# The last two chunks of a graph kernel's first edge pass, in an order written out by hand on TensorE, VectorE and ScalarE

## The chip, the cores and the metric

The kernel runs on one core of one Trainium2 chip. The metric is the device time of one execution in microseconds (us), as the median of several runs. TensorE is PE in the profile, VectorE is DVE, ScalarE is ACT, GpSimd is POOL and SyncE is SP. Each engine has its own instruction stream, and the streams meet at semaphores.

## The reference

Two graph layers follow each other on 3125 nodes with 64 channels and 100000 edges sorted by destination, each with a residual and a layer norm. The first layer is what the change touches:

```python
h1, h2, h3, h4 = (_node_proj(x, W, b, node_type) for W, b in ...)
w5e = einsum('mf,mfh->mh', edge_feat, W5[edge_type]) + b5[edge_type]
num = sum(h3[edge_dst] * (h4[edge_src] + w5e), axis=-1)
score = softmax((num / sqrt(16))[:, None], axis=-1)[:, 0]
msg = score[:, None] * (h2[edge_src] + w5e)
out = h1 + segment_sum(msg, edge_dst, num_segments=n)
...
x = layernorm(x + out)
```

The second layer gathers the rows of this new `x` by `edge_src`, so nothing of it can be gathered before the first layer's sums are complete.

## The kernel before, in words

The program has a preparation, an edge pass over 98 chunks (stage 0, the first layer), a short part on the nodes (sums of each node fetched, layer norm), a second edge pass over 98 chunks (stage 1, the second layer) and an end part. A chunk is 512 edges of the first half of the edge list beside 512 of the second half, so that 128 partitions hold two times 64 channels. Chunk c has the parity s = c % 2 and the round r = c // 2; most tiles exist twice, one for each parity, and semaphores of the pair count rounds. The last two chunks are 96 (s = 0) and 97 (s = 1).

In stage 0 a chunk goes through these steps, each a function called with `chunk_of(c)`:

- POOL, `gather0` (L509): six or eight indirect DMAs of rows into a ring of eight buffers (`rows0_0`, `rows0_1`, and six in `block1`, which the profile prints as `rows` and `block`).
- PE, `project0`: one matmul of the masked features by `w5` (L779, printed as x2), then the gathered rows are transposed and added to it (L753, L758), which is what `q4_ready` announces; and the start values `inj` are transposed (L788, `injT`).
- DVE, `products`: a scan that carries the row of h3 from edge to edge (L1078, `h3_ready`, needs `injT`), then the product with `q_sum` (L1083, `prod_ready`, needs `q4_ready`).
- PE, `numerator` (L805) transposes the product, and `difference` (L753, L758) adds the other half of the rows to `q_sum`.
- DVE, `score_parts` (L1057, L1060, L1063): sums of channels, maximum, difference. ACT, `exponents` (L598). DVE, `probabilities` (L1088, L1090, L1093). ACT, `widen` (L604), spreads the probability over the channels. PE, `turn_prob` (L814), transposes it.
- DVE, `message_sums` (L1099, L1105): the product with `q2_sb` (copied by ACT, `copy_q2`, L617) and the scan of sums, `run`. It needs `keep_late`, which ACT copies in `copy_keep` (L611).
- PE, `turn_run` (L825), transposes `run`. ACT, `store0` (L628, L630), copies it and issues the store to `d_run0`.

The order on each engine is that in which the code calls the functions: a loop over c with offsets, so that in one turn an engine works on up to four neighbouring chunks. DVE's turn c is `score_parts(c-1)`, `mask(c+1)`, `products(c)`, `probabilities(c-1)`, `message_sums(c-2)`; PE's is `project0(c+1)`, `numerator(c)`, `difference(c)`, `turn_prob(c-1)`, `turn_run(c-2)`; ACT's is `exponents(c-1)`, `copy_keep(c)`, `widen(c-1)`, `copy_q2(c)`, `store0(c-2)`. In every turn but the last ones PE also does 75 matmuls of `pick0` (L770) and DVE some 12 comparisons (L1051) for the rows that are picked by matmul instead of gathered.

When all stores of stage 0 have landed, POOL fetches the sums of each node (L541, 25 indirect DMAs), DVE and ACT norm them in five groups, SP writes `d_x1`, and POOL's gathers of stage 1 (`gather1`, L519) start.

Of the kernel before, what the change touches and what calls it, by code (L numbers as in the profile page):

```python
# [33 lines left out]
CHUNKS = 2 * -(-N_EDGES // (4 * CH))  # L34
# [36 lines left out]
def gnn_program(nc, t, out):  # L71
# [3 lines left out]
    with ctx:  # L75
# [221 lines left out]
        def chunk_of(c):  # L297
            return (c % 2, c // 2, c) if 0 <= c < CHUNKS else None

        def tiles_of(c):  # L300

            return PE_J if c % 2 == 0 else TILES
# [8 lines left out]
        def wait(eng, semaphore, count):  # L311

            if count > 0:
                eng.wait_ge(semaphore, count)
# [247 lines left out]
        def _(act):  # L562
# [56 lines left out]
            def copy_picked(u):  # L619

                act.wait_ge(picked[u % 2], u // 2 + 1)
                wait(act, q2_ready[0], u - 1)
                act.activation(picked_sb[u % 2], p_pick[u % 2], ACT.Copy).then_inc(own_ready[u % 2], 1)

            def store0(s, r, c):
                act.wait_ge(runT[s], r + 1)
                wait(act, stored[s], 16 * r)
                act.activation(stage0[s][:, :, :].rearrange("p j c -> p (j c)"), p_out0[:, :], ACT.Copy).then_inc(staged[s], 1)  # L628
                act.wait_ge(staged[s], r + 1)
                act.dma_start(d_run0[bass.ds(2 * CH * c, 2 * CH), :].rearrange("(p j h) c -> p j (h c)", j=TILES, h=2),  # L630
                              stage0[s][:, :, :]).then_inc(stored[s], 16)

            copy_picked(0)
            for c in range(CHUNKS + 2):
                for work, d in ((exponents, -1), (copy_keep, 0), (widen, -1), (copy_q2, 0)):
                    if chunk_of(c + d):
                        work(*chunk_of(c + d))
                if c % 2 == 0 and c // 2 + 1 < PICKS:
                    copy_picked(c // 2 + 1)
                if chunk_of(c - 2):  # L640
                    store0(*chunk_of(c - 2))

            def square_and_root(g, first):

                act.wait_ge(s_square, first + g + 1)
                act.activation(sq[:, g * GT:(g + 1) * GT, :], centred[:, g * GT:(g + 1) * GT, :], ACT.Square).then_inc(s_squared, 1)
                act.wait_ge(s_var, first + g + 1)
                act.activation(std[:, g * GT:(g + 1) * GT], var[:, g * GT:(g + 1) * GT], ACT.Sqrt).then_inc(s_sqrt, 1)
# [72 lines left out]
        def _(pe):  # L721
# [27 lines left out]
            def add_rows(s, c, which):  # L749

                rows = [ring[c % RING][:, j, :, :].rearrange("p h c -> p (h c)") for j in range(TILES)]
                for j in range(tiles_of(c)):
                    ins = pe.matmul(q_sum[s][:, j:CH:TILES], rows[j][:, which:4 * C:2], ident[:, :], is_transpose=True,  # L753
                                    start=False, stop=True, skip_group_check=True)
                if c % 2 == 0:
                    u = c // 2
                    for h in range(2):
                        ins = pe.matmul(q_sum[s][:, PE_J:CH:TILES], sel[:, which, (1 - h) * C:(3 - h) * C], picked_sb[u % 2][:, h * P:(h + 1) * P],  # L758
                                        start=False, stop=True, skip_group_check=True)
                return ins  # L760
# [14 lines left out]
            def project0(s, r, c):  # L775

                pe.wait_ge(masked[s], r + 1)
                wait(pe, q2_copied[s], r)
                pe.matmul(q_sum[s], w5[:, :], featm[s][:, :], start=True, stop=True)  # L779
                pe.wait_ge(got_rows[c % RING], 16 * 2 * tiles_of(c) * (c // RING + 1))  # L780
                if c % 2 == 0:
                    pe.wait_ge(own_ready[c // 2 % 2], c // 4 + 1)
                add_rows(s, c, 1).then_inc(q4_ready[s], 1)
                pe.wait_ge(inj_in[s], 16 * (r + 1))
                if c > 0:
                    pe.wait_ge(h3_ready[1 - s], r + s)
                for j in range(TILES):
                    ins = pe.matmul(p_inj[:, j:CH:TILES], inj[s][:, j, :], ident[:, :], is_transpose=True,  # L788
                                    start=True, stop=True)
                ins.then_inc(injT[s], 1)  # L790
# [38 lines left out]
            pe.wait_ge(s_left, 2)  # L829
            for half in range(2):  # L830
                pick0(0, half)
            for c in range(-1, CHUNKS + 2):
                u, half = (c + 3) // 2, (c + 3) % 2
                if u < PICKS:
                    pick0(u, half)
                for work, d in ((project0, 1), (numerator, 0), (difference, 0), (turn_prob, -1), (turn_run, -2)):
                    if chunk_of(c + d):
                        work(*chunk_of(c + d))

            def project1(s, r, c):  # L840

# [75 lines left out]
        def _(dve):  # L917
# [126 lines left out]
            def one_hot0(u, half):  # L1044

                s = u % 2
                if half == 0:
                    dve.wait_ge(slots_in[u % PICK_SLOTS], 16 * (u // PICK_SLOTS + 1))
                    wait(dve, picked[s], u // 2)
                for k in range(half * NT_FIRST, NT if half else NT_FIRST):  # L1050
                    ins = dve.tensor_scalar(hot0[s][:, k, :], pick_slots[u % PICK_SLOTS][0:NP, :], pick_of[:, k:k + 1], None, ALU.is_equal)  # L1051
                ins.then_inc(hot_ready[s], 1)
# [16 lines left out]
                dve.scalar_tensor_tensor(featm[s][:, :], types[s][:, :], type_of_row[:, :], feat[s][:, :],  # L1069
                                         ALU.is_equal, ALU.mult).then_inc(masked[s], 1)  # L1070

            def products(s, r, c):

                dve.wait_ge(keep_in[s], 32 * (r + 1))
                dve.wait_ge(injT[s], r + 1)
                if c > 0:
                    dve.wait_ge(h3_ready[1 - s], r + s)
                dve.tensor_tensor_scan(h3d[s][:, :], keep[s][:, :], p_inj[:, :], h3d[1 - s][:, CH - 1:CH],  # L1078
                                       ALU.mult, ALU.add).then_inc(h3_ready[s], 1)
                dve.wait_ge(h3_ready[s], r + 1)  # L1080
                dve.wait_ge(q4_ready[s], r + 1)
                wait(dve, num_ready[s], r)
                dve.scalar_tensor_tensor(prod[s][:, :], h3d[s][:, :], 0.25, q_sum[s], ALU.mult, ALU.mult).then_inc(prod_ready[s], 1)  # L1083
# [23 lines left out]

            for u, half in ((0, 0), (0, 1), (1, 0)):
                one_hot0(u, half)
            for c in range(-1, CHUNKS + 2):  # L1110
                for work, d in ((score_parts, -1), (mask, 1), (products, 0), (probabilities, -1), (message_sums, -2)):
                    if chunk_of(c + d):
                        work(*chunk_of(c + d))
                u, half = (c + 4) // 2, c % 2
                if u < PICKS:
                    one_hot0(u, half)

            def layer_norm(src, g, first):

# [205 lines left out]
```

## Time and profile before

| | |
|---|---|
| median of 3 runs | 1893.9 us (1891.12 to 1894.66) |
| profiled execution, its own time | 1900.41 us |
| its span in the trace | 1898.6 us |
| busy: PE, DVE, POOL, ACT | 1611.0, 1673.0, 1334.5, 758.3 us |
| mean granted TensorE clock | 0.952 of full speed |

The span is the time from the first to the last instruction in the trace; times in the trace's rows count from its start. The profiled execution is 1.8 us longer than its span and 6.5 us longer than the median of the runs. Busy shares are means over stages with different limits. For a change at one place only that place's rows tell what is waited for.

### The profile page before, as it was taken

To read this page: it belongs to the slowest core of one execution; us is meant where nothing else is said; L and a number is where in the kernel's file an instruction comes from. 1 tells how busy PE (TensorE), PEld (TensorE's weight loads), DVE (VectorE), ACT (ScalarE), POOL (GpSimd) and SP (SyncE) were. 2 spreads that over 40 slices of the span, in tenths; PEclk is the share of its full clock that TensorE was granted. 3 is DMA by queue.
4 is the path that set the end of the run, shared out by engine and by line. 5 is a ranking of instruction groups with operands and counts; after the bars stand their busy time and mean duration, and the time that the engine had idled before them with its cause. 6 is when DMAs were issued, how large, how long until landed. Compare 5 with 4: busy or idle time off the path is not lost.

```text
span 1898.6 us, 32478 instructions
## 1 busy us (share of the span) xinstructions
PE 1611.0 (85%) x10331; PEld 1182.0 (62%) x10331; DVE 1673.0 (88%) x3845; ACT 758.3 (40%) x1438; POOL 1334.5 (70%) x1391
## 2 busy tenths in 40 slices
PE   4406999999999999999982399999999999999936
PEld 3305888888888888888772155555555555555525
DVE  4333999999999999999987589999999999999976
ACT  3100233332323333233321156665665665665632
POOL 3557777777777777777773677777777777777742
PEclk9998999999999999999996699999999999999955
DMA  9782555556565665655552256666666666666631
GB/s 288 233 327 86 167 168 173 171 172 178 166 177 169 171 177 167 178 163 173 165 161 55 58 145 187 189 184 181 177 189 187 187 185 183 176 190 184 182 101 38
DMA packets 220337, 323.22 MB, mean 170 GB/s; under 512 B 65697, under 2 KB 127706, under 8 KB 220039
## 3 DMA queue, kind: packets, MB, share of 16 engines
q1 hardware_dynamic: 116096, 146.04, 25.2%
q0 software_dynamic: 44464, 70.87, 17.9%
q10 hardware_dynamic: 59608, 104.24, 15.2%
q8 instruction: 84, 1.38, 0.3%
q14 instruction: 85, 0.70, 0.1%
HBM read 186.93 MB, written 134.02 MB: 169 GB/s over the span
## 4 chain that ended last, share of the span: by engine, by line
POOL 61%; issue 21%; PE 6%; DVE 5%; DMA 4%; SPq 2%; ACT 1%; ACTq 0%; DVEq 0%; POOLq 0%
POOL rows L519 29%; POOL block L509 22%; POOL rows L509 8%; PE bank L729 2%; POOL typed L541 1%; DMA d_inj<-zeros 1%; POOL d_inj L532 1%; SPq L387 1%; PE wide L912 1%; PE wide L770 1%; DMA w_nodes<-in_b 1%; DVE edge_lists L1051 1%; DVE h3d L1078 0%; DVE run L1105 0%; DVE late L1051 0%
## 5 line engine op out<-in xcount | busy, mean ns | idle before, releaser
L519 POOL DMA_INDIRECT rows<-d_x,idx x588 | 557.2, 948 | 189.2 <-issue 179.0
L509 POOL DMA_INDIRECT block<-d_h,idx x504 | 490.6, 973 | 153.7 <-issue 153.4
L866 PE MATMUL wide<-late,ntype_i 125*128 125x512 bf16 x975 | 220.8, 382 | 51.5 <-DVE ntype_i L1180 51.5
L770 PE MATMUL wide<-late,typed 125*128 125x256 bf16 x1250 | 209.6, 274 | 62.7 <-DVE late L1051 62.6
L611 ACT ACTIVATE keep_late<-keep 128x512 bf16<-128x512 bf16 x98 | 61.8, 630 | 428.8 <-DVE run L1105 428.8
L509 POOL DMA_INDIRECT rows<-d_h,idx x182 | 176.7, 971 | 70.5 <-issue 55.2
L866 PE MATMUL wide<-edge_lists,ntype_i 125*128 125x512 bf16 x936 | 210.0, 379 | 0.0
L770 PE MATMUL wide<-edge_lists,typed 125*128 125x256 bf16 x1200 | 201.6, 275 | 3.8 <-DVE edge_lists L1051 3.3
L866 PEld LDWEIGHTS wide<-late,ntype_i 125*128 125x128 bf16 x975 | 96.3, 99 | 157.9 <-DVE ntype_i L1180 51.9
L877 PE MATMUL wide<-ident,block 128*128 128x128 f32 x784 | 141.8, 306 | 38.3 <-DVE block L1220 29.5
L770 PEld LDWEIGHTS wide<-late,typed 125*128 125x128 bf16 x1250 | 120.3, 98 | 82.3 <-issue 59.0
L770 PE MATMUL wide<-late,ntype_i 125*128 125x256 bf16 x625 | 171.2, 274 | 0.0
L770 PE MATMUL wide<-edge_lists,ntype_i 125*128 125x256 bf16 x600 | 164.5, 274 | 0.0
L866 PEld LDWEIGHTS wide<-edge_lists,ntype_i 125*128 125x128 bf16 x936 | 92.1, 98 | 100.0
L877 PEld LDWEIGHTS wide<-ident,block 128*128 128x128 f32 x784 | 110.3, 209 | 62.5 <-DVE block L1220 47.4
L1078 DVE TENSOR_TENSOR_SCAN h3d<-keep,h3d,bank 128x512 f32<-128x512 bf16 x98 | 124.8, 1274 | 25.5 <-PE bank L788 25.5
L680 ACT ACTIVATE bank<-prob_wide 128x512 f32<-128x512 f32 x98 | 59.0, 602 | 214.1 <-DVE block L1220 210.7
L1051 DVE TENSOR_SCALAR late<-zeros,pick_of 125x256 bf16<-125x256 f16 x625 | 128.3, 299 | 4.0 <-DMA zeros<-d_pick 4.0
L770 PEld LDWEIGHTS wide<-edge_lists,typed 125*128 125x128 bf16 x1200 | 115.5, 99 | 23.2 <-DVE edge_lists L1051 9.4
L1195 DVE TENSOR_TENSOR_SCAN h3d<-bank,h3d,keep 128x511 f32<-128x511 f32 x98 | 125.5, 1281 | 3.5
L1105 DVE TENSOR_TENSOR_SCAN run<-keep_late,run,bank 128x512 f32<-128x512 bf16 x98 | 125.4, 1280 | 3.5
L1215 DVE TENSOR_TENSOR_SCAN block<-bank,block 128x512 f32<-128x512 f32 x98 | 124.3, 1268 | 1.1 <-ACT bank L680 1.1
(207 smaller groups left out, 3453.7 us busy)
## 6 DMA issues: line engine op xcount, KB each, us to landing
d_run<-block ACTq DMA_DIRECT2D x98, 512.0 KB
d_inj<-zeros SPq DMA_DIRECT2D x28, 896.0 KB, 16.9
inj<-d_inj SPq DMA_DIRECT2D x98, 256.0 KB
d_run<-stage ACTq DMA_DIRECT2D x98, 256.0 KB
feat<-in_ea16x3T SPq DMA_DIRECT2D x196, 96.0 KB
types<-d_type SPq DMA_DIRECT2D x196, 64.0 KB
keep<-d_keep SPq DMA_DIRECT2D x196, 64.0 KB
keep<-d_pen SPq DMA_DIRECT2D x196, 64.0 KB
```

What stands on the lines that cost most here:

```text
L509: pool.indirect_dma_start(out=ring[c % RING][:, j, h, :], out_offset=None, in_=d_h24, in_offset=bass.IndirectOffsetOnAxis(ap=idx[:, c, at: ...
L519: pool.indirect_dma_start(out=rows1[c % RING1][:, j, h, :], out_offset=None, in_=d_x1, in_offset=bass.IndirectOffsetOnAxis(ap=idx[:, c, at ...
L611: act.activation(keep_late[s][:, :], keep[s][:, :], ACT.Copy).then_inc(keep_copied[s], 1)
L680: act.activation(p_decay[:, :], up[s], ACT.Exp, scale=-1.0).then_inc(decay_ready[s], 1)
L770: ins = pe.matmul(p_pick[s], table0[n][:, k, :], hot0[s][:, k, :], start=(k == 0 and n == 0), stop=(k == NT - 1 and n == 2), skip_group_ch ...
L866: ins = pe.matmul(p_hot[s], table[q][:, SPLIT * k:SPLIT * (k + 1), :].rearrange("p b c -> p (b c)"), hot[s][:, k, :], start=(k == 0 and q ...
L877: ins = pe.matmul(p_out1[:, q * CH + j * P:q * CH + (j + 1) * P], src[:, j:CH:TILES], ident[:, :], is_transpose=True, start=True, stop=True)
L1051: ins = dve.tensor_scalar(hot0[s][:, k, :], pick_slots[u % PICK_SLOTS][0:NP, :], pick_of[:, k:k + 1], None, ALU.is_equal)
L1078: dve.tensor_tensor_scan(h3d[s][:, :], keep[s][:, :], p_inj[:, :], h3d[1 - s][:, CH - 1:CH], ALU.mult, ALU.add).then_inc(h3_ready[s], 1)
L1105: dve.tensor_tensor_scan(run[s][:, :], keep_late[s][:, :], p_prob[:, :], run[1 - s][:, CH - 1:CH], ALU.mult, ALU.add).then_inc(run_ready[s ...
L1195: dve.tensor_tensor_scan(before[s][:, 1:CH], p_m[c % 3][:, 0:CH - 1], keep[s][:, 1:CH], before[s][:, 0:1], ALU.max, ALU.add).then_inc(befo ...
L1215: dve.tensor_tensor_scan(run_s[s][:, :], p_decay[:, :], expm[s][:, :], run_s[1 - s][:, CH - 1:CH], ALU.mult, ALU.add).then_inc(s_run[s], 1)
```

## The change

The three loops end two turns earlier on their upper side and the last turns are written out as one list for each engine; `CHUNKS - back` is the chunk, so back 1 is chunk 97 and back 2 is chunk 96. Two functions are split so that their halves can stand apart: `turn_inj` is the second half of `project0`, and `expand` is the first half (the scan of h3) of `products`. Up to and with turn 95 each engine's order is as it was. No instruction is added or removed.

```diff
@@ ScalarE
-            for c in range(CHUNKS + 2):
+            for c in range(CHUNKS - 2):
...
+            for work, back in ((exponents, 3), (copy_keep, 2), (widen, 3), (copy_q2, 2), (store0, 4), (exponents, 2), (widen, 2),
+                               (copy_keep, 1), (copy_q2, 1), (exponents, 1), (store0, 3), (widen, 1), (store0, 2), (store0, 1)):
+                work(*chunk_of(CHUNKS - back))
@@ TensorE
                 add_rows(s, c, 1).then_inc(q4_ready[s], 1)
+
+            def turn_inj(s, r, c):
+
                 pe.wait_ge(inj_in[s], 16 * (r + 1))
...
-            for c in range(-1, CHUNKS + 2):
+            for c in range(-1, CHUNKS - 2):
...
-                for work, d in ((project0, 1), (numerator, 0), (difference, 0), (turn_prob, -1), (turn_run, -2)):
+                for work, d in ((project0, 1), (turn_inj, 1), (numerator, 0), (difference, 0), (turn_prob, -1), (turn_run, -2)):
...
+            for work, back in ((numerator, 2), (difference, 2), (turn_prob, 3), (turn_run, 4), (turn_inj, 1), (project0, 1),
+                               (turn_prob, 2), (numerator, 1), (difference, 1), (turn_run, 3), (turn_run, 2), (turn_prob, 1), (turn_run, 1)):
+                work(*chunk_of(CHUNKS - back))
@@ VectorE
-            def products(s, r, c):
+            def expand(s, r, c):
...
+            def products(s, r, c):
+
                 dve.wait_ge(h3_ready[s], r + 1)
...
-            for c in range(-1, CHUNKS + 2):
-                for work, d in ((score_parts, -1), (mask, 1), (products, 0), (probabilities, -1), (message_sums, -2)):
+            for c in range(-1, CHUNKS - 2):
+                for work, d in ((score_parts, -1), (mask, 1), (expand, 0), (products, 0), (probabilities, -1), (message_sums, -2)):
...
+            for work, back in ((score_parts, 3), (mask, 1), (expand, 2), (products, 2), (probabilities, 3), (message_sums, 4),
+                               (score_parts, 2), (expand, 1), (probabilities, 2), (message_sums, 3), (products, 1),
+                               (message_sums, 2), (score_parts, 1), (probabilities, 1), (message_sums, 1)):
+                work(*chunk_of(CHUNKS - back))
```

On PE, behind `turn_run` of chunk 93 (which is the transpose of `run1`), the program before goes on with the matmul of chunk 97's features by `w5` and its last gathered rows (`rows0_1`), and only then with chunk 96's numerator (`prod0`):

```order
L825 MATMUL bank3<-ident,run1 128x128 x4
L779 MATMUL wide0<-featm1,w5 128x512
L753 MATMUL wide0<-ident,rows0_1 128x128 x4
L788 MATMUL bank0<-ident,inj1 128x128 x4
L805 MATMUL bank1<-ident,prod0 128x128 x4
L753 MATMUL wide0<-ident,rows0_0 128x128 x3
L758 MATMUL wide0<-msg1,sel 128x128 x2
L814 MATMUL bank2<-ident,prob_wide1 128x128 x4
L825 MATMUL bank3<-ident,run0 128x128 x4
```

The same place in the changed program (its line numbers are higher by 3 to 6: L820 is `turn_prob`, L831 `turn_run`, L811 `numerator`, L794 `turn_inj`, L782 the matmul by `w5`):

```order
L831 MATMUL bank3<-ident,run1 128x128 x4
L811 MATMUL bank1<-ident,prod0 128x128 x4
L756 MATMUL wide0<-ident,rows0_0 128x128 x3
L761 MATMUL wide0<-msg1,sel 128x128 x2
L820 MATMUL bank2<-ident,prob_wide1 128x128 x4
L831 MATMUL bank3<-ident,run0 128x128 x4
L794 MATMUL bank0<-ident,inj1 128x128 x4
L782 MATMUL wide0<-featm1,w5 128x512
L756 MATMUL wide0<-ident,rows0_1 128x128 x4
```

All of chunk 97's PE work has moved behind the four pieces that belong to chunks 94, 95 and 96, and the transpose of `inj1` stands ahead of chunk 97's rows.

On DVE, behind `message_sums` of chunk 94 (`run0`), the program before has chunk 96's scores, chunk 97's scan and product, chunk 96's probabilities and chunk 95's message sums (`run1`):

```order
L1057 TENSOR_REDUCE score0<-bank1 128x8
L1060 TENSOR_REDUCE top0<-score0 128x8
L1063 TENSOR_TENSOR diff0<-score0,top0 128x8
L1078 SCALAR_TENSOR_TENSOR h3d1<-keep1,h3d0,bank0 128x512
L1083 SCALAR_TENSOR_TENSOR prod1<-h3d1,wide0 128x512
L1088 TENSOR_REDUCE total0<-expo0 128x8
L1090 RECIPROCAL inv0<-total0 128x8
L1093 TENSOR_TENSOR prob0<-expo0,inv0 128x8
L1099 TENSOR_TENSOR bank2<-bank2,q2_sb1 128x512
L1105 SCALAR_TENSOR_TENSOR run1<-keep_late1,run0,bank2 128x512
L1057 TENSOR_REDUCE score1<-bank1 128x8
```

The same place in the changed program (L1087 is the scan of h3, L1095 the product, L1111 and L1117 are `message_sums`):

```order
L1066 TENSOR_REDUCE score0<-bank1 128x8
L1069 TENSOR_REDUCE top0<-score0 128x8
L1072 TENSOR_TENSOR diff0<-score0,top0 128x8
L1087 SCALAR_TENSOR_TENSOR h3d1<-keep1,h3d0,bank0 128x512
L1100 TENSOR_REDUCE total0<-expo0 128x8
L1102 RECIPROCAL inv0<-total0 128x8
L1105 TENSOR_TENSOR prob0<-expo0,inv0 128x8
L1111 TENSOR_TENSOR bank2<-bank2,q2_sb1 128x512
L1117 SCALAR_TENSOR_TENSOR run1<-keep_late1,run0,bank2 128x512
L1095 SCALAR_TENSOR_TENSOR prod1<-h3d1,wide0 128x512
L1111 TENSOR_TENSOR bank2<-bank2,q2_sb0 128x512
L1117 SCALAR_TENSOR_TENSOR run0<-keep_late0,run1,bank2 128x512
```

The product of chunk 97 has moved behind `run1` of chunk 95, and chunk 96's message sums stand ahead of chunk 97's scores.

On ACT, the program before from the exponentials of chunk 96 (`expo0`) to the end of the stage:

```order
L598 ACTIVATE expo0<-diff0 128x8
L611 ACTIVATE keep_late1<-keep1 128x512
L604 ACTIVATE prob_wide0<-prob0 128x512
L617 ACTIVATE q2_sb1<-wide0 128x512
L628 ACTIVATE stage0_1<-bank3 128x512
L630 DMA d_run0<-stage0_1 128x512
L598 ACTIVATE expo1<-diff1 128x8
L604 ACTIVATE prob_wide1<-prob1 128x512
```

And in the changed program, with the same line numbers:

```order
L598 ACTIVATE expo0<-diff0 128x8
L604 ACTIVATE prob_wide0<-prob0 128x512
L611 ACTIVATE keep_late1<-keep1 128x512
L617 ACTIVATE q2_sb1<-wide0 128x512
L598 ACTIVATE expo1<-diff1 128x8
L628 ACTIVATE stage0_1<-bank3 128x512
L630 DMA d_run0<-stage0_1 128x512
L604 ACTIVATE prob_wide1<-prob1 128x512
```

Chunk 96's probabilities no longer stand behind the copy of `keep_late1`, and chunk 97's exponentials stand ahead of the store of chunk 95.

## Rows read from the trace of the kernel before

**Rows 1.** The page, part 4: the chain that ended last, by engine.

```profile
POOL 61%; issue 21%; PE 6%; DVE 5%; DMA 4%; SPq 2%; ACT 1%; ACTq 0%; DVEq 0%; POOLq 0%
```

**Rows 2.** The page, part 5, stage 1's gathers: busy, mean ns | idle before.

```profile
L519 POOL DMA_INDIRECT rows<-d_x,idx x588 | 557.2, 948 | 189.2 <-issue 179.0
```

**Rows 3.** The timeline of POOL around the end of stage 0: start, duration (us).

```profile
999.29 0.95 POOL L509 DMA_INDIRECT rows<-d_h,idx  x1 [0.30 <-issue]
...
1028.85 0.95 POOL L541 DMA_INDIRECT typed<-d_run,last_i  x1 [28.61 <-DMA d_run<-stage]
...
1073.14 1.08 POOL L519 DMA_INDIRECT rows<-d_x,idx  x1 [10.21 <-DMA d_x<-typed]
```

**Rows 4.** The timeline of PE in the loop of stage 0.

```profile
973.50 1.02 PE L779 MATMUL wide<-featm,w 128*128 128x512 f32 x2
...
975.46 0.60 PE L788 MATMUL bank<-ident,inj 128*128 128x128 f32 x4
975.90 0.65 PE L805 MATMUL bank<-ident,prod 128*128 128x128 f32 x4
976.38 0.64 PE L753 MATMUL wide<-ident,block 128*128 128x128 f32 x4
```

**Rows 5.** The timeline of PE at the end of stage 0.

```profile
1003.82 1.13 PE L753 MATMUL wide<-ident,rows 128*128 128x128 f32 x4 [5.72 <-DMA rows<-d_h,idx]
1004.75 1.06 PE L788 MATMUL bank<-ident,inj 128*128 128x128 f32 x4
1005.60 1.06 PE L805 MATMUL bank<-ident,prod 128*128 128x128 f32 x4
...
1021.10 1.09 PE L814 MATMUL bank<-ident,prob_wide 128*128 128x128 f32 x4 [4.17 <-DVE run L1105]
...
1024.30 1.13 PE L825 MATMUL bank<-ident,run 128*128 128x128 f32 x4 [1.25 <-DVE run L1105]
```

**Rows 6.** The timeline of DVE at the end of stage 0.

```profile
998.15 0.69 DVE L1083 SCALAR_TENSOR_TENSOR prod<-h3d,wide 128x512 f32<-128x512 f32 x1
...
999.99 1.28 DVE L1105 TENSOR_TENSOR_SCAN run<-keep_late,run,bank 128x512 f32<-128x512 bf16 x1
1006.70 0.69 DVE L1057 TENSOR_REDUCE score<-bank 128x8 f32<-128x512 f32 x1 [5.43 <-PE bank L805]
...
1011.14 0.16 DVE L1088 TENSOR_REDUCE total<-expo 128x8 f32<-128x8 f32 x1 [1.41 <-ACT expo L598]
...
1011.58 0.17 DVE L1093 TENSOR_TENSOR prob<-expo,inv 128x8 f32<-128x8 f32 x1
...
1012.39 1.28 DVE L1105 TENSOR_TENSOR_SCAN run<-keep_late,run,bank 128x512 f32<-128x512 bf16 x1
1013.59 0.67 DVE L1057 TENSOR_REDUCE score<-bank 128x8 f32<-128x512 f32 x1
...
1014.48 0.17 DVE L1063 TENSOR_TENSOR diff<-score,top 128x8 f32<-128x8 f32 x1
...
1022.23 0.70 DVE L1099 TENSOR_TENSOR bank<-bank,q_sb 128x512 f32<-128x512 f32 x1 [1.27 <-PE bank L814]
1022.96 1.28 DVE L1105 TENSOR_TENSOR_SCAN run<-keep_late,run,bank 128x512 f32<-128x512 bf16 x1
```

**Rows 7.** The timeline of ACT at the end of stage 0 (ACTq: its DMA issue).

```profile
1001.90 0.61 ACT L604 ACTIVATE prob_wide<-prob 128x512 f32<-128x512 f32 x1
...
1009.90 0.60 ACT L628 ACTIVATE stage<-bank 128x512 f32<-128x512 f32 x1 [1.11 <-PE bank L825]
...
1010.90 0.21 ACT L598 ACTIVATE expo<-diff 128x8 f32<-128x8 f32 x1 [0.40 <-ACT stage L628]
...
1026.09 0.33 ACTq L630 DMA_DIRECT2D d_run<-stage  x1
```

**Rows 8.** Stretches of 1 us: length, busy of PE, PEld, DVE, ACT, POOL, granted clock, DMA share, GB/s.

```profile
1004.00:1005.00 1.00, 1.00 (x6) 1.00 (x7) 0.00 (x0) 0.00 (x0) 0.00 (x0) 0.50 0.00 0
...
1010.00:1011.00 1.00, 1.00 (x8) 0.82 (x7) 0.00 (x0) 0.60 (x2) 0.00 (x0) 1.00 0.00 0
```

## The prediction

> **What bounds the kernel now.** I read the chain that ended last first: POOL and the time in which it merely issues are most of it [rows 1]. Stage 1's gathers explain why: POOL sat idle for 189.2 us around them, 179.0 us of it plain issue time [rows 2], and the remaining 10.2 us is one wait, that of its first gather for `d_x1` at 1073.14 [rows 3]. So in stage 1 POOL never waits for another engine, and whatever lets it start earlier is kept to the end. In front of it POOL stands still for 28.61 us, from its last gather of stage 0 (999.29) to its first fetch of node sums (1028.85), which waits for the last store [rows 3]. This hole is what the change can shorten. What fills it is read from the timelines of PE, DVE and ACT.
>
> The last gathered rows let PE go on at 1003.82 after 5.72 us of idleness [rows 5]. In those 5.72 us chunk 96's product was long there (998.15 plus 0.69, so 998.84 [rows 6]), but its numerator stood behind chunk 97's rows and started at 1005.60 [rows 5]. Hence DVE got chunk 96's scores to work on at 1006.70, after 5.43 us idle [rows 6]. Its exponentials then stood behind a store on ACT (copy at 1009.90, exponentials 1.00 us later, at 1010.90 [rows 7]), and DVE took them up at 1011.14 [rows 6]. Chunk 97's way from there was message sums at 1022.23, last transpose 1024.30, last store issued at 1026.09 [rows 5 to 7].
>
> **The change, step by step.** Nothing is added; instructions trade places. I follow the changed order with durations of the rows, twice: at full TensorE clock and at half. A group of four transposes starts 0.46 us after the one before at full clock (975.46, 975.90, 976.38) and itself lasts 0.60 to 0.65 [rows 4]; at half clock the pace is 0.86 (0.93 and 0.85 in the rows) and the length 1.06 to 1.13 [rows 5]. Below, the first number is full clock, the second half.
>
> 1. Up to DVE's `run` of chunk 94 all is as before: it ends at 999.99 + 1.28 = 1001.27 [rows 6].
> 2. PE does chunk 96's numerator at 998.90, as soon as the product is there, inside the wait for rows. Done by 999.6 or 1000.0. Its cover is that wait; without it, it would cost one group.
> 3. DVE takes chunk 96's scores right behind 1001.27; maximum and difference end 1.06 us later (1013.59 to 1014.65 [rows 6]), at 1002.33. Before, this began at 1006.70.
> 4. ACT's `widen` of chunk 95 ends at 1002.51, unmoved [rows 7]. PE: `turn_prob(95)` 1002.57, `turn_run(94)` 1003.03 / 1003.43, `turn_inj(97)` 1003.49 / 1004.29, ending 1004.09 / 1005.35. Behind it the matmul by `w5`: 1.05 us at full clock (1.02 plus issue [rows 4]); at half clock the trace has none, and I bound it between 1.05 and twice that. Then chunk 97's rows, which have landed at 1003.82 anyway, ready at 1005.65 / 1008.40. Before, they were added from 1003.82.
> 5. This is the wait that is added: DVE's scan `expand(97)` needs `turn_inj(97)`, and `probabilities(96)` and `message_sums(95)` are queued behind it. It starts at 1004.12 / 1005.38 and ends 1.28 us later, 1005.40 / 1006.66. DVE idles some 2 to 3 us there.
> 6. ACT stores chunk 94 from 1003.72 / 1004.53, and its exponentials of chunk 96 end 1.21 us later, 1004.93 / 1005.74. That is under the scan of step 5, so the store ahead of them costs nothing here; had the scan ended earlier, 0.9 us would show.
> 7. DVE needs 2.53 us from chunk 96's total to the end of chunk 95's `run` (1011.14 to 1012.39 + 1.28 [rows 6]): 1007.93 / 1009.19. Chunk 97's product follows with 0.69: 1008.62 / 1009.88. Its rows were ready 2.3 / 0.8 us before, so the late `w5` stays hidden, at either bound.
> 8. `widen(96)` ends at 1006.67 / 1007.9 and PE waits for `run` of chunk 95: `turn_prob(96)` 1008.05 / 1009.30, ending 1008.65 / 1010.39. DVE's `message_sums(96)` takes 2.01 (1022.23 to 1024.24 [rows 6]): 1010.69 / 1012.43. PE meanwhile does numerator and difference of 97 and `turn_run(95)`, until 1010.25 / 1012.94.
> 9. Scores of 97, 1.06: 1011.75 / 1013.49. Exponentials: 1011.99 / 1013.73. Now ACT stores chunk 95 in front of `widen(97)`, again 1.00 us [rows 7], of which DVE's probabilities (0.61, 1011.14 to 1011.75 [rows 6]) hide 0.6. `widen(97)` ends 1013.63 / 1015.37.
> 10. `turn_prob(97)` from 1013.69 / 1015.43, 0.60 / 1.09 long; `message_sums(97)` 2.01 plus 0.03: 1016.33 / 1018.56; last `turn_run` 0.06 later, 0.65 / 1.13 long: 1017.04 / 1019.75; store issued 0.66 later (1025.43 to 1026.09 [rows 5, 7]): 1017.70 / 1020.41.
>
> Against 1026.09 that is 8.4 us earlier at full clock throughout and 5.7 us at half clock throughout.
>
> **Which clock.** In the trace the granted clock was 0.50 (1.2 GHz) at 1004 to 1005, after PE had stood idle for 5.72 us, and back at 1.00 (2.4 GHz) at 1010 to 1011, after it had worked from 1003.82 on [rows 5, 8]. In the changed order the long hole has chunk 96's numerator and difference in it, and the next work starts at 1002.57. So I take full clock up to `turn_run(95)`, and half clock for the last three groups, which stand between gaps of 2 us and more as those at 1021.10 and 1024.30 did (1.09 and 1.13 us long [rows 5]). That is the full-clock line until `turn_prob(97)`, plus 0.49 on it and 0.48 on the last `turn_run`: issued at 1018.67, 7.4 us earlier.
>
> The Trainium skill speaks against this choice: its page TensorE: Matmul & The Clock Gate, in Part 4 on PE-mode transpose, says that transposes don't count as PE activity and don't bring the full clock. Here the work from 1003.82 to 1010 was nearly all transposes, and the clock did come back [rows 5, 8]; by that rule the gain would be the 5.7 us of the half-clock line.
>
> **What follows.** From the store's issue to POOL's first fetch (2.76 us) and on, everything hangs on stage 0's end: POOL on the last store, DVE on the end of its last `run`, which moves by the same 7.4 us (1024.24 to 1016.82). Stage 1 never makes POOL wait [rows 2]. So the 7.4 us pass in full. The sum stands against the profiled execution (1900.41 us, span 1898.6 us), which is 6.5 us longer than the median of the runs; a shift at one place should be the same in both: 1893.9 - 7.4 = 1886.5 us, a ratio of 0.996. What a measurement can tell from no change is about 0.2%, 3.8 us here.
>
> **Rivals.**
> - **Half clock throughout**: 5.7 us earlier, 1888.2 us. For it: all work in this stretch comes in pieces with gaps of 1 to 2 us, and the clock was low at 1004. Against it: it had recovered by 1010 with gaps no shorter than those after. Chance 0.33.
> - **The gain is given back inside the stage** (within 0.2%): the new wait of step 5 lasts longer. If `turn_inj(97)` comes 1.9 us or more later than in the half-clock line, less than 3.8 us is left, since DVE has no slack behind it. What could delay it is only `turn_prob(95)`, which waits for `widen(95)`, unmoved in the trace. At 3 us late it gives 1891.2 us. A miss of small waits that I counted at 0.03 to 0.1 us ends here too. Chance 0.12.
> - **Slower**: the same wait, grown past the whole gain. `expand(97)` holds DVE's queue, behind it `message_sums(95)`, for which PE's `turn_prob(96)` waits, in front of the numerator of 97. From 5.7 + 3.8 = 9.5 us of delay on (injected rows at about 1014.9) the kernel is slower by over 0.2%, 1897.7 us or more. Against it: in the trace `inj` of chunk 97 was transposed at 1004.75 without a wait of its own [rows 5]. Chance 0.03.
> - **Full clock throughout**: 8.4 us, 1885.5 us. Chance 0.07, and 0.45 for the forecast.
>
> **The numbers.** The likeliest gives 1886.5 us; full and half clock give 1885.5 and 1888.2. The three runs of before lie within 3.5 us, so each end gets 1.5 to 2 us more: 1884.0 to 1890.5. That leaves out the two cases in which the wait grows, 0.15. Faster 0.85, within 0.2% 0.12, slower 0.03.
>
> **What would show it.** In the new trace: chunk 96's numerator near 998.9; DVE's scores near 1001.3 with no 5.43 us hole in front; a DVE hole of 1.7 to 3 us in front of chunk 97's scan, released by the transpose of `inj`; exponentials of 96 at about 1005; the last store at 1018.7 and POOL's first fetch at 1021.4; granted clock 1.00 around 1005 to 1010. I am wrong if that scan starts after 1006, if chunk 97's product waits for its rows (step 7), or if POOL waits anywhere in stage 1.

## The result and the profile after

The changed kernel takes 1888.55 us (median of 8 runs, 1886.8 to 1889.33) against 1893.95 us (8 runs, 1891.12 to 1895.8): 5.4 us less, ratio 0.9972 with a 95% interval of 0.9963 to 0.9981, which is 3.6 to 7.0 us. It is faster: the interval does not reach a ratio of 1, though its near end (0.19%) is no more than the 0.2% that I had called the least that can be told apart. The forecast was 1886.5 us. One execution of e4 below (2762.79 us, granted clock 0.588) and one of the kernel before on the third chip (2363.5 us, 0.735) were slow ones and stand outside the ratios.

The timeline of PE in the changed kernel, from chunk 96's numerator on (L811 numerator, L820 `turn_prob`, L831 `turn_run`, L794 `turn_inj`, L782 the matmul by `w5`; start and duration in us):

```profile
997.03 0.75 PE L811 MATMUL bank<-ident,prod 128*128 128x128 f32 x4 [1.65 <-DVE prod L1095]
...
1000.71 0.66 PE L820 MATMUL bank<-ident,prob_wide 128*128 128x128 f32 x4 [2.12 <-ACT prob_wide L604]
...
1001.80 1.06 PE L794 MATMUL bank<-ident,inj 128*128 128x128 f32 x4
...
1002.65 1.91 PE L782 MATMUL wide<-featm,w 128*128 128x512 f32 x2
...
1006.80 0.63 PE L820 MATMUL bank<-ident,prob_wide 128*128 128x128 f32 x4 [1.54 <-DVE run L1117]
...
1012.32 1.12 PE L820 MATMUL bank<-ident,prob_wide 128*128 128x128 f32 x4 [0.16 <-ACT prob_wide L604]
...
1015.55 1.13 PE L831 MATMUL bank<-ident,run 128*128 128x128 f32 x4 [2.11 <-DVE run L1117]
```

The timeline of DVE in the same stretch (L1087 scan of h3, L1117 scan of sums):

```profile
998.14 1.28 DVE L1117 TENSOR_TENSOR_SCAN run<-keep_late,run,bank 128x512 f32<-128x512 bf16 x1
999.33 0.67 DVE L1066 TENSOR_REDUCE score<-bank 128x8 f32<-128x512 f32 x1
...
1002.95 1.28 DVE L1087 TENSOR_TENSOR_SCAN h3d<-keep,h3d,bank 128x512 f32<-128x512 bf16 x1 [2.56 <-PE bank L794]
...
1005.37 1.28 DVE L1117 TENSOR_TENSOR_SCAN run<-keep_late,run,bank 128x512 f32<-128x512 bf16 x1
1006.57 0.66 DVE L1095 SCALAR_TENSOR_TENSOR prod<-h3d,wide 128x512 f32<-128x512 f32 x1
...
1014.21 1.28 DVE L1117 TENSOR_TENSOR_SCAN run<-keep_late,run,bank 128x512 f32<-128x512 bf16 x1
```

And those of ACT and POOL:

```profile
1003.04 0.21 ACT L598 ACTIVATE expo<-diff 128x8 f32<-128x8 f32 x1 [0.40 <-ACT stage L628]
...
1017.34 0.33 ACTq L630 DMA_DIRECT2D d_run<-stage  x1
...
1020.11 0.94 POOL L541 DMA_INDIRECT typed<-d_run,last_i  x1 [21.72 <-DMA d_run<-stage]
```

Chunk 96's numerator starts at 997.03, before POOL has even issued its last gather (997.44), DVE goes from chunk 94's sums into chunk 96's scores without a gap (5.43 us of idleness before, [rows 6]), and POOL waits 21.72 us instead of 28.61 [rows 3]: 6.89 us less. The new wait stands where it was expected, 2.56 us in front of chunk 97's scan, released by the transpose of `inj`.

From here on I compare by one length, called the way: from the end of chunk 94's `run`, up to which the orders are equal, to the issue of the last store. Before it was 1026.09 - 1001.27 = 24.82 us [rows 6, 7], now it is 1017.34 - 999.42 = 17.92 us, 6.90 less.

The two traces' spans differ by more, 1898.6 - 1886.9 = 11.7 us. POOL's rows divide it: 1.85 us lie ahead of POOL's last gather of stage 0 (999.29 and 997.44), 6.89 in the wait, 1.87 between the first fetch of sums and the first gather of stage 1 (1028.85 to 1073.14 [rows 3] and 1020.11 to 1062.53), 1.09 behind. The third of these is no effect of the change: the kernels e1 to e4 below needed 42.4 to 42.9 us there, whether they gained anything or not, and the kernel before itself 42.6 and 42.5 in its two later traces (e9, f4); its first trace, with 44.3, was the odd one.

### The profile page after: what moved, and what is told of

Same layout as the page of the kernel before. It is cut to its first block, busy times and chain, and to the rows that moved or that the text cites. A ratio compares the mean times of both kernels' runs of the same rounds, so it can differ in the third digit from the quotient of the medians.

```text
span 1886.9 us, 32478 instructions
## 1 busy us (share of the span) xinstructions
PE 1609.1 (85%) x10331; PEld 1178.7 (62%) x10331; DVE 1669.8 (88%) x3845; ACT 758.1 (40%) x1438; POOL 1335.3 (71%) x1391
## 4 chain that ended last, share of the span: by engine, by line
POOL 62%; issue 21%; PE 6%; DVE 4%; DMA 3%; SPq 2%; ACT 1%; ACTq 0%; DVEq 0%; POOLq 0%
POOL rows L519 29%; POOL block L509 23%; POOL rows L509 7%; PE bank L732 2%; POOL typed L541 1%; DMA d_inj<-zeros 1%; POOL d_inj L532 1%; SPq L387 1%; PE wide L921 1%; PE wide L773 1%; DMA w_nodes<-in_b 1%; DVE h3d L1087 0%; DVE run L1117 0%; DVE edge_lists L1060 0%; DVE typed L961 0%
## 5 line engine op out<-in xcount | busy, mean ns | idle before, releaser
L1087 DVE TENSOR_TENSOR_SCAN h3d<-keep,h3d,bank 128x512 f32<-128x512 bf16 x98 | 124.8, 1274 | 28.0 <-PE bank L794 28.0
L1117 DVE TENSOR_TENSOR_SCAN run<-keep_late,run,bank 128x512 f32<-128x512 bf16 x98 | 125.4, 1280 | 3.5
```

The costliest lines, as they stand in the source:

```text
L1117: dve.tensor_tensor_scan(run[s][:, :], keep_late[s][:, :], p_prob[:, :], run[1 - s][:, CH - 1:CH], ALU.mult, ALU.add).then_inc(run_ready[s ...
```

## The experiments

They ran on three further chips. On chip 2 (e1 to e4) the kernel before has a median of 1899.59 us. On chips 3 and 4 it takes 2313 us; what the traces show of that, without its cause, stands at the end. The comparisons there are within the same chip, and the changed kernel itself was not run on these two. In the table, run 95 and run 96 are the ends of these scans, counted like the way from the end of chunk 94's.

| kernel | chip | ratio to before (95%) | run 95 | run 96 | way, us |
|---|---|---|---|---|---|
| before | 1 | | 12.40 | 19.69 | 24.82 |
| changed | 1 | 0.9972 (0.9963 to 0.9981) | 7.23 | 10.06 | 17.92 |
| e1 changed again | 2 | 0.9967 (0.9954 to 0.9979) | 7.06 | 9.88 | 17.75 |
| e2 ACT's old order | 2 | 0.9983 (0.9974 to 0.9992) | 7.91 | 12.37 | 20.48 |
| e3 DVE's old order | 2 | 0.9989 (0.9981 to 0.9998) | 9.90 | 15.69 | 21.63 |
| e4 PE's old order | 2 | 1.0000 (0.9991 to 1.0009) | 11.33 | 16.85 | 24.71 |
| before (e9) | 3 | | 6.25 | 13.54 | 18.67 |
| e5 inj early | 3 | 1.0000 (0.9985 to 1.0015) | 6.94 | 9.77 | 17.20 |
| e6 and exponentials | 3 | 0.9975 (0.9962 to 0.9989) | 4.63 | 7.66 | 15.52 |
| e7 and `w5` | 3 | 0.9980 (0.9965 to 0.9995) | 5.37 | 8.27 | 16.13 |
| before (f4) | 4 | | 6.24 | 12.70 | 17.84 |
| f2 inj early | 4 | 0.9997 (0.9986 to 1.0007) | 7.07 | 10.05 | 17.45 |
| f1 and exponentials | 4 | 0.9985 (0.9974 to 0.9997) | 4.62 | 8.40 | 15.80 |
| f3 changed, gaps filled | 4 | 0.9986 (0.9977 to 0.9995) | 8.07 | 10.90 | 17.93 |

**e1: the changed kernel again.** No edit.

> The changed kernel once more, unaltered. My theory: POOL's wait between its last gather of stage 0 and its first fetch of node sums, 28.61 us before and 21.72 us in the first trace of the changed kernel, is again within 0.7 us of 21.7 (the rest is at which moment the TensorE clock falls), and the 6.9 us saved there pass in full to the end: ratio about 0.9964. Rival: part of the saving is given back behind the stage, 1 to 2 us, and the ratio stays near 0.9972 with the wait still at 21.7.

The way is 17.75 us, and the ratio gives 6.3 us (4.0 to 8.7). POOL's wait was 22.80 us, outside the 0.7 us that I had allowed, only because it also holds the time from its last gather to the end of chunk 94's `run`, which varies with how far the other engines are behind: 998.52 to 1000.80 here, 998.39 to 999.42 in the first trace. The way is the cleaner measure.

**e2: ACT's order of before**, the other two as changed:

```diff
-                               (copy_keep, 1), (copy_q2, 1), (exponents, 1), (store0, 3), (widen, 1), (store0, 2), (store0, 1)):
+            ... (exponents, 2), (copy_keep, 1), (widen, 2), (copy_q2, 1), (store0, 3),
+                               (exponents, 1), (widen, 1), (store0, 2), (store0, 1)):
```

> ScalarE's order of before, the others as changed. My theory: the copy of keep_late of chunk 97, which waits for run of chunk 95, stands again ahead of chunk 96's widen, so turn_prob(96) comes about 1.1 us later; the store of chunk 95 ahead of chunk 97's exponentials costs nothing more. POOL's wait 22.8 us, time 1 us above the changed kernel. Rival, ScalarE's order is what brings the gain: POOL's wait 25 us or more.

The way is 20.48 us, 2.7 more than e1, where I expected 1.0. POOL's wait, 23.05 us, looks like a hit (22.8) by luck: chunk 94's `run` ended 0.2 us ahead of the last gather's end here and 2.3 us behind it in e1. The timeline of ACT and PE in e2:

```profile
1004.17 0.63 ACT L611 ACTIVATE keep_late<-keep 128x512 bf16<-128x512 bf16 x1 [3.49 <-DVE run L1118]
1004.71 0.61 ACT L604 ACTIVATE prob_wide<-prob 128x512 f32<-128x512 f32 x1
1005.38 1.11 PE L821 MATMUL bank<-ident,prob_wide 128*128 128x128 f32 x4 [3.67 <-ACT prob_wide L604]
...
1009.09 0.60 ACT L628 ACTIVATE stage<-bank 128x512 f32<-128x512 f32 x1 [0.26 <-PE bank L832]
...
1010.09 0.21 ACT L598 ACTIVATE expo<-diff 128x8 f32<-128x8 f32 x1 [0.40 <-ACT stage L628]
```

`widen(96)`, ready since 1002.2, stands behind the copy that waits for chunk 95's `run`, and `turn_prob(96)` starts 1.3 us after that scan ends (1004.08) instead of 0.15 us after it: the expected 1.1 us. The store of chunk 95 did cost something: the exponentials of chunk 97, ready at 1009.52, ran at 1010.09. The rest is TensorE's clock: it was at half from 993.5 to 1000.4, so that chunk 95's `run` ended 0.85 us later than in e1, and at half again for `turn_prob(96)` (1.11 us against 0.63). The 0.85 us are no effect of ACT's order, which is the same up to there.

**e3: DVE's order of before.** The chunk 97 product stands again in front of chunk 96's probabilities, chunk 96's message sums behind chunk 97's probabilities:

```diff
-                               (score_parts, 2), (expand, 1), (probabilities, 2), (message_sums, 3), (products, 1),
-                               (message_sums, 2), (score_parts, 1), (probabilities, 1), (message_sums, 1)):
+                               (score_parts, 2), (expand, 1), (products, 1), (probabilities, 2), (message_sums, 3),
+                               (score_parts, 1), (probabilities, 1), (message_sums, 2), (message_sums, 1)):
```

> VectorE's order of before, the others as changed. My theory: chunk 97's product stands ahead of chunk 96's probabilities and waits for chunk 97's rows (about 1 us), and chunk 96's message sums stand behind chunk 97's exponentials: the end of the last run moves by 2.3 us. POOL's wait 24.0 us, a third of the gain lost. Rival: without VectorE's order TensorE's brings nothing, wait 28 us.

The timeline of DVE in e3:

```profile
1004.43 0.69 DVE L1095 SCALAR_TENSOR_TENSOR prod<-h3d,wide 128x512 f32<-128x512 f32 x1 [1.29 <-PE wide L756]
...
1009.02 0.69 DVE L1066 TENSOR_REDUCE score<-bank 128x8 f32<-128x512 f32 x1 [1.46 <-PE bank L811]
```

The product waits 1.29 us for chunk 97's rows, as expected. DVE then stands idle for 1.46 us in front of chunk 97's scores, with chunk 96's sums queued behind them: chunk 97's product is ready at 1005.12, but on PE its numerator stands behind `turn_prob(96)`, which starts when chunk 95's `run` is done, at 1007.70. The way is 21.63, 3.9 above e1, where I expected 2.3, and POOL's wait 26.29 us instead of 24.0. I had not counted the second wait. Here too 0.85 us is the clock, at half from 995 to 1005: DVE waited 3.23 us for the injected rows, against 2.38 in e1, ahead of the point where the orders part.

**e4: PE's order of before**, the other two as changed:

```diff
-            for work, back in ((numerator, 2), (difference, 2), (turn_prob, 3), (turn_run, 4), (turn_inj, 1), (project0, 1),
-                               (turn_prob, 2), (numerator, 1), (difference, 1), (turn_run, 3), (turn_run, 2), (turn_prob, 1), (turn_run, 1)):
+            for work, back in ((project0, 1), (turn_inj, 1), (numerator, 2), (difference, 2), (turn_prob, 3), (turn_run, 4),
+                               (numerator, 1), (difference, 1), (turn_prob, 2), (turn_run, 3), (turn_prob, 1), (turn_run, 2), (turn_run, 1)):
```

> TensorE's order of before, the others as changed. My theory: chunk 96's numerator waits again behind chunk 97's rows, VectorE stands idle some 5.4 us in front of chunk 96's scores as before, and the other two engines' orders can't make up for it, since run of chunk 95 then ends when it did: POOL's wait 28 to 30 us, no gain at all, perhaps 1 us of loss. Rival: each engine's order brings a share of its own: wait 24 to 26 us.

The timeline of PE and DVE in e4:

```profile
1006.98 1.13 PE L756 MATMUL wide<-ident,rows 128*128 128x128 f32 x4 [4.66 <-DMA rows<-d_h,idx]
...
1008.75 1.06 PE L811 MATMUL bank<-ident,prod 128*128 128x128 f32 x4
...
1009.85 0.69 DVE L1066 TENSOR_REDUCE score<-bank 128x8 f32<-128x512 f32 x1 [4.37 <-PE bank L811]
```

Nothing is gained: way 24.71 us, POOL's wait 30.49 us, ratio 1.0000. The numerator of chunk 96 is again behind the rows of chunk 97, and DVE idle for it. The rival, a share for each engine, falls: the shares are not additive. Without PE's order the other two bring nothing; with it, the traces give DVE's order 3.9 us and ACT's 2.7, or 3.0 and 1.9 without the 0.85 us of clock. PE's new order alone, with both others old, was not run.

These four also bear on whether the gain passes on. From e1 to e2, e3 and e4 the way grows by 2.7, 3.9 and 7.0 us, the medians (1893.14, 1895.72, 1897.17, 1900.64) by 2.6, 4.0 and 7.5. From the last store's issue to the end of the span the traces need 869.5 to 872.5 us on chips 1 and 2, without relation to the gain (before 872.5, changed 869.6, e1 871.7, e4 871.7). So nothing is seen to be given back behind the stage, but a loss of 1 us would not show. Single executions differ by more in front of the way: the traced one of e2, at 1888.3 us, was 3.7 us shorter than that of e1 although its way was 2.7 us longer, since its chunk 94 was done 4.6 us earlier. Only the medians can be set beside the ways.

**e5, f2: the new wait, taken away.** On PE `turn_inj` of chunk 97 goes ahead of `turn_prob` of chunk 95:

```diff
-            for work, back in ((numerator, 2), (difference, 2), (turn_prob, 3), (turn_run, 4), (turn_inj, 1), (project0, 1),
+            for work, back in ((numerator, 2), (difference, 2), (turn_inj, 1), (turn_prob, 3), (turn_run, 4), (project0, 1),
```

> TensorE alone: chunk 97's turn_inj stands right behind chunk 96's difference, ahead of turn_prob(95), instead of behind turn_run(94). Measured is the way from the end of run of chunk 94 to the issue of the last store (24.82 us before, 17.92 and 17.75 us changed). My theory, from step 5 and 6 of the prediction: VectorE's wait in front of chunk 97's scan (2.4 to 2.6 us) goes, but then it waits for chunk 96's exponentials, which stand behind the store of chunk 94 on ScalarE: only about 0.9 us is gained, way 17.0 us. Rival, the wait for the injected rows is paid in full: way 15.4 us.

> The kernel with turn_inj alone moved, once more, for the same reason. My theory: way 17.0 us, VectorE waiting for chunk 96's exponentials instead of the injected rows. Rival: 15.5 us, as with the exponentials moved too.

Both ran on chips of the 2313 us kind, where POOL had issued its last gather 45 us and more ahead of chunk 94's end, so that no rows are waited for. The way is 17.20 and 17.45 us, where I expected 17.0. DVE's wait for the injected rows has gone, and in its place stands one for the exponentials, here in e5:

```profile
1269.33 0.16 DVE L1100 TENSOR_REDUCE total<-expo 128x8 f32<-128x8 f32 x1 [2.20 <-ACT expo L598]
```

That is step 6 of the prediction seen from the other side: with the scan early, the store in front of the exponentials shows. The time is that of the kernel before within the intervals; its own way is 18.67 and 17.84 us on these chips, so little was to be had.

**e6, f1: both taken away.** In addition, on ACT:

```diff
-            ... (copy_q2, 2), (store0, 4), (exponents, 2), (widen, 2),
+            ... (copy_q2, 2), (exponents, 2), (store0, 4), (widen, 2),
```

> The same and, on ScalarE, chunk 96's exponentials ahead of the store of chunk 94. My theory: both covers are gone, the scan and the exponentials are early, 2.4 us gained against the changed kernel: way 15.4 us, up to 0.7 us more where TensorE is at half clock and chunk 97's rows become late for its product. Rival: no better than with the injected rows alone (17.0 us), since chunk 97's rows, which landed about 2.5 us after the end of run of chunk 94, become what is waited for.

> The kernel with chunk 97's turn_inj right behind chunk 96's difference and chunk 96's exponentials ahead of the store of chunk 94, once more, since the chip of its first run held TensorE back all along (2313 us for the kernel before) and showed a way of 15.52 us there. My theory: on a chip like the first two the way is 15.3 to 15.9 us from the end of run of chunk 94 to the last store, about 2.2 us below the changed kernel, ratio to before about 0.9955. Rival: chunk 97's rows, which land late here and had landed long before on that chip, become what is waited for, way 17 us or more.

Chunk 95's `run` ends 4.6 us after chunk 94's, 2.3 and 2.45 us earlier than in e5 and f2, and the way is 15.52 and 15.80 us. In f1, at half clock, chunk 97's product did wait for its rows' transposes, by 1.16 us:

```profile
1271.55 0.69 DVE L1095 SCALAR_TENSOR_TENSOR prod<-h3d,wide 128x512 f32<-128x512 f32 x1 [1.16 <-PE wide L756]
```

This is the shortest way of all, with ratios to before of 0.9975 and 0.9985. The question of f1, how it does where the last rows land late, stays open: the chip was again not of that kind. For the same reason, and since the changed kernel was not run on these chips, I can't say that this version beats it.

**e7: `w5` in the hole.** `project0` is split, and its matmul by `w5` stands behind `turn_inj`, ahead of `turn_prob` of chunk 95; the rows are added where `project0` stood.

```diff
+            def project_rows(s, r, c):
...
+            for work, back in ((numerator, 2), (difference, 2), (turn_inj, 1), (project0, 1), (turn_prob, 3), (turn_run, 4), (project_rows, 1),
```

> The same again and, on TensorE, chunk 97's matmul by w5 split off from the addition of its rows and done in the wait in front of turn_prob(95). My theory: it takes 1 to 1.9 us out of the way to chunk 97's product, which matters only if its rows were what was waited for: way 15.2 us, or like the run before. It also fills TensorE's hole, so the clock may stay up longer; that would show as 1.0 of granted clock around chunk 97's numerator.

A miss: 16.13 us, 0.6 longer than e6. PE's hole in front of `turn_prob(95)` was 0.46 us in e6, and the matmul by `w5` took 1.91 us at half clock. `turn_prob(95)` came 1.0 us later, counted from chunk 94's `run`, and DVE stood 0.65 us idle in front of chunk 95's sums:

```profile
1266.21 0.70 DVE L1114 TENSOR_TENSOR bank<-bank,q_sb 128x512 f32<-128x512 f32 x1 [0.65 <-PE bank L823]
```

The clock was at 1.00 around chunk 97's numerator in e6 and in e7, and fell 9.8 and 9.9 us behind chunk 94's `run`: the filled hole did not keep it up longer.

**f3: PE kept busy**, the changed kernel with matmuls of constants into an unused bank:

```diff
+            def busy(count):
+                for n in range(count):
+                    pe.matmul(p_pick[0][:, 0:P], w5[:, :], ident[:, :], start=True, stop=True, skip_group_check=True)
...
                 work(*chunk_of(CHUNKS - back))
+                busy({(difference, 2): 6, (project0, 1): 4, (turn_run, 3): 6, (turn_prob, 1): 6}.get((work, back), 0))
```

> The changed kernel with 22 matmuls of constants added in TensorE's idle gaps of the last two chunks (6 behind chunk 96's difference, 4 behind chunk 97's rows, 6 behind turn_run(95), 6 behind turn_prob(97)); they write an unused bank and change no result. My theory, from the two lines of the prediction: the clock stays at 1.00, and the way comes down from 17.9 toward the full-clock line, 16.4 to 17.0 us. Rival: the clock falls anyway, or the added matmuls run at half clock and push the real ones, way 18 us or more.

The timeline of PE in f3 (L837 are the added ones; the profile prints each of these f32 matmuls as two):

```profile
1260.50 2.76 PE L837 MATMUL wide<-ident,w 128*128 128x128 f32 x12
1263.06 1.04 PE L820 MATMUL bank<-ident,prob_wide 128*128 128x128 f32 x4
...
1274.46 0.66 PE L820 MATMUL bank<-ident,prob_wide 128*128 128x128 f32 x4 [0.28 <-ACT prob_wide L604]
...
1277.22 0.75 PE L831 MATMUL bank<-ident,run 128*128 128x128 f32 x4 [0.77 <-DVE run L1122]
```

And two of its stretches of 1 us, granted clock third from the end:

```profile
1260.00:1261.00 1.00, 1.00 (x7) 1.00 (x6) 1.00 (x2) 0.19 (x1) 0.00 (x0) 0.50 0.97 354
1264.00:1265.00 1.00, 1.00 (x10) 1.00 (x9) 0.00 (x0) 0.41 (x1) 0.00 (x0) 1.00 0.00 0
```

Each theory got half. The first six ran at half clock, 2.76 us, and pushed `turn_prob(95)`, so chunk 95's `run` ended at 8.07. From 1264 on the clock was at 1.00 in every stretch, and the last two groups took 0.66 and 0.75 us instead of 1.12 and 1.13: from `run` 95 to the store 9.86 us, against 10.69 both in the changed kernel and in e1. In sum 17.93 us, nothing won. Its ratio on that chip, 0.9986, is better than its way against f4's (17.84) explains; I have no cause for that.

**e9, f4: the kernel before again**, for its way.

> The kernel before, unaltered, for a second trace of it. The first had a way of 24.82 us from the end of run of chunk 94 to the last store, while the times differ by 5.4 and about 6.3 us only, not 6.9 to 7.1. If the way is 23.5 to 24.5 us here, the difference is how the TensorE clock happened to fall in the first trace; if it is 24.8 again, 0.6 to 1.5 us are given back behind the stage.

> The kernel before, for a second trace on such a chip. If its way is 23.5 to 24.3 us instead of 24.82, the two traces' difference of 6.9 us overstated the gain by how the clock fell, and the 5.4 to 6.3 us of the times are the whole of it. If it is 24.8 again, something of the gain is given back behind the stage.

Neither answers its question, since on these chips the rows that the old order waits for have long landed: 18.67 and 17.84 us say what the old order costs without that wait. They suggest something else, as far as chips can be compared: of the 24.8 us on the first chip some 6 to 7 (24.82 less 18.67 or 17.84) are that wait, the same size as the gain.

## Why the prediction was right, and where it was off

- What bounds the kernel: right. PE's order in front of the last rows is the cause, shown by e4, and POOL never waits in stage 1: in the traces of before and of the changed kernel 587 of its 588 gathers there have only issue time in front of them, and the first one its wait for `d_x1`. That the gain passes on is shown by e1 to e4 to within about 1 us.
- Steps 2 and 3, numerator and scores of chunk 96: counted from the end of `run` 94 they came within 0.1 us of the sum.
- Step 5, the added wait: right in place and length (2.56 us). That `inj` of chunk 97 would be late, my rival for "no change" and "slower", did not happen.
- Step 4 and the choice of the clock: here the sum was off. I took full clock up to `turn_run(95)`. It fell to half (1.2 GHz) at about 1001.5 already, for 3.4 us, after PE had stood idle for 1.65 us in front of 997.03 and for 2.12 us in front of 1000.71 (the 1 us stretches of the changed kernel, granted clock third from the end):

```profile
1001.00:1002.00 1.00, 1.00 (x9) 1.00 (x8) 0.00 (x0) 0.14 (x1) 0.00 (x0) 0.77 0.00 0
1002.00:1003.00 1.00, 1.00 (x6) 0.99 (x5) 0.05 (x1) 0.60 (x1) 0.00 (x0) 0.50 0.00 0
...
1005.00:1006.00 1.00, 0.25 (x2) 0.01 (x1) 0.96 (x2) 0.39 (x1) 0.00 (x0) 1.00 0.00 0
```

  so that `turn_inj` took 1.06 us and ended 0.6 us later than the full-clock line has it, and everything behind it moved. My argument for full clock there, that in the trace of before it had recovered by 1010 with gaps no shorter, misread the rows: from 1003.82 to 1011 PE had worked without any gap. The way came out at 17.92 us where the sum had 17.40, and 19.14 for half clock throughout. The matmul by `w5` took 1.91 us there, inside the bounds of 1.05 and 2.1, and was hidden: the rows were ready at 1005.25, the product started at 1006.57.
- Step 6, the store ahead of chunk 96's exponentials: right, they ended at 1003.25, under the scan, which ended at 1004.23.
- Step 7, that chunk 97's product would not wait for its rows: right, and e3 and f1 show the price when it does (1.29 and 1.16 us).
- Steps 8 to 10: right within 0.15 us once the 0.5 us of the clock are taken off; the last two groups ran at half clock, 1.12 and 1.13 us, as chosen. f3, on another chip, measured what that costs, 0.83 us against my 0.97.
- The size: 7.4 us forecast, 6.9 in the traces, 5.4 (3.6 to 7.0) and 6.3 (4.0 to 8.7) in the times. The difference between 6.9 and 5.4 is within the intervals. Whether the first trace's 24.82 us was typical for before is open: e4, with the same order on PE, had 24.71, but a second trace of before on such a chip is missing.
- The clock rule of the Trainium skill (TensorE: Matmul & The Clock Gate, Part 4), that transposes don't bring the full clock, is not borne out: in the trace of before, between 1003.82 and 1010, the only work that is no transpose is one group of picked rows (1.06 us), and the clock rose [rows 5, 8]; the same order did the same in e4. A stretch of transposes alone that shows it I have not. In the changed kernel the clock rose again before 1005, there with the `w5` matmul among the work. By that rule the gain would have been 5.7 us, nearer to the median of the times than my sum, but not by that mechanism: the groups of chunks 96 and 97 at 1006.80 to 1009 took 0.63 to 0.75 us.

## What to carry to other kernels

At the end of a pipelined loop the steady order makes finished work stand behind work that waits for the last transfer; look for an engine that idles for a DMA while its next-but-one instruction has long been ready. Change the order first on the engine that waits for the transfer (here PE): without it the better orders of the others brought nothing, and with it leaving one of them out cost 3.9 and 2.7 us, of which 0.85 us each was the clock. Then follow each remaining wait, since taking one away shows the next (the injected rows, then the store in front of the exponentials), and don't fill a hole with more than it holds (e7, f3).

## What the hardware showed that I had not expected

**The clock is part of such a tail.** The way from `run` 95 to the store was 10.69 us in two traces and 12.6 in e2, where ACT's order cost 1.6 to 1.7 of it; the rest came from which of four or five small PE groups fell into half clock. Terms of 0.5 us each are decided by that, so a forecast of such a stretch to better than 1 us isn't to be had from the order alone.

**Two of four chips ran the same program in 2313 us instead of 1894 or 1900.** The stretch from 300 to 900 us, first the kernel before on the first chip, then on the third (length, busy us and instructions of PE, PEld, DVE, ACT, POOL, granted clock, DMA share, GB/s):

```profile
300.00:900.00 600.00, 583.20 (x4666) 502.88 (x4665) 583.31 (x1650) 188.34 (x387) 456.96 (x470) 1.00 0.60 172
```

```profile
300.00:900.00 600.00, 512.36 (x3596) 426.85 (x3594) 454.44 (x1274) 144.54 (x297) 361.66 (x380) 0.89 0.46 134
```

TensorE got through 3596 matmuls instead of 4666. Every 20 to 23 us it issues single matmuls with gaps of 0.3 to 2 us and nothing to wait for (timeline of PE in e9); in the traces of before and of e1 there is no such gap between 900 and 1000 us:

```profile
1144.33 0.28 PE L758 MATMUL wide<-msg,sel 128*128 128x128 f32 x1
1145.66 0.39 PE L758 MATMUL wide<-msg,sel 128*128 128x128 f32 x2 [1.05 <-issue]
1147.15 0.35 PE L758 MATMUL wide<-msg,sel 128*128 128x128 f32 x1 [1.10 <-issue]
```

The clock falls to half behind such a gap (0.50 from 1149 to 1151 in e9), and the other engines wait for TensorE: POOL, which never did in stage 1 on the first chip, stood 53.6 us there behind PE in e9. In the three traces of e9, f1 and f4 the last such gap of stage 0 lies at 1214 to 1220 us, 2.6 to 2.9 us behind the start of POOL's last gather, and none follows in the next 40 us. Whether the gathers have to do with it was not tried. On such a chip PE bounds the kernel and not POOL, and a change that shortens a wait for POOL's rows has nothing to shorten.
